# An attention kernel's score chunks: an even issue order, and the causal bar added by VectorE within its maximum

## The reference

```
Q, K, V = relu(xn @ W + b)                  # 16 heads of 8 channels
scores  = Q K^T / sqrt(8)                   # 512 x 512 per head and batch
scores  = -2^32 + 1 where the key is masked or lies behind the query
out     = softmax(scores) V + xn, then a layer norm with gamma and beta
```

## Time and profile before

| | us |
|---|---|
| median of three runs | 537.47 (536.09 to 538.89) |
| the profiled execution, its own time | 538.71 |
| its span in the trace | 536.9 |

### The profile page before, as it was taken

How to read it: one execution, slowest core, us unless ns; L and a number is a source line. 1 busy time by engine, 2 the same in 40 slices (tenths; PEclk the granted TensorE clock), 3 DMA queues, 4 the chain that set the end, 5 groups by cost and what they waited for, 6 DMA issues and landing times.

```text
span 536.9 us, 10757 instructions
## 1 busy us (share of the span) xinstructions
PE 447.4 (83%) x3773; PEld 275.3 (51%) x3773; DVE 406.4 (76%) x1008; ACT 315.3 (59%) x670; POOL 124.7 (23%) x345
## 2 busy tenths in 40 slices
PE   0049545988999739999999999999999999999981
PEld 0026334766777515565555555555556556556540
DVE  6898988887884238576977877877878878887715
ACT  0029135977888803566656666656667567566670
POOL 8000000000000011001045045045054063072181
PEclk9999958989999955799999999999999999999997
DMA  8900021223333351122122222322212213212000
GB/s 220 295 20 0 20 80 43 75 80 98 98 98 88 110 146 22 47 76 62 56 83 67 72 67 66 85 56 66 85 53 77 82 46 93 64 48 69 2 21 20
DMA packets 28585, 39.68 MB, mean 74 GB/s; under 512 B 5751, under 2 KB 19959, under 8 KB 28535
## 3 DMA queue, kind: packets, MB, share of 16 engines
q1 hardware_dynamic: 28486, 39.03, 26.0%
q10 hardware_dynamic: 48, 0.01, 0.0%
HBM read 25.91 MB, written 10.49 MB: 68 GB/s over the span
## 4 chain that ended last, share of the span: by engine, by line
PE 55%; DVE 6%; issue 1%; ACT 1%; DVEq 0%; ACTq 0%
PE banks L979 15%; PE banks L1010 14%; PE banks L998 13%; PE banks L981 6%; PE banks L1000 5%; DVE mx L837 3%; PE banks L1020 3%; DVE stats L879 1%; DVE aggr L883 1%; ACT pt L950 0%; ACT ots L934 0%; PE banks L988 0%; DVE res L866 0%; DVE res L869 0%; DVE mixed L870 0%
## 5 line engine op out<-in xcount | busy, mean ns | idle before, releaser
L837 DVE TENSOR_REDUCE mx<-banks 128x1 f32<-128x384 f32 (+3 forms) x384 | 212.5, 598 | 59.7 <-PE banks L981 52.5
L950 ACT ACTIVATE pt<-banks 128x512 f32<-128x512 f32 (+2 forms) x384 | 184.8, 528 | 110.4 <-PE banks L1000 104.1
L981 PE MATMUL banks<-causal,ident_b 128*128 128x128 bf16 x512 | 106.8, 228 | 0.0
L1000 PE MATMUL banks<-causalT,ident_b 128*128 128x128 bf16 x512 | 103.7, 222 | 0.0
L979 PE MATMUL banks<-w_room 73*128 73x512 bf16 (+3 forms) x256 | 75.3, 331 | 11.5 <-DVEq L912 10.3
L1010 PE MATMUL banks<-pt,vg 128*9 128x512 f32 (+3 forms) x1024 | 81.9, 438 | 0.5 <-ACT pt L950 0.5
L998 PE MATMUL banks<-w_room 76*128 76x512 bf16 (+3 forms) x256 | 71.2, 310 | 0.0
L979 PE MATMUL banks<-k_odd,q_odd 73*128 73x512 bf16 (+3 forms) x256 | 69.0, 302 | 1.6 <-DVE mx L837 1.6
L998 PE MATMUL banks<-q_odd,k_odd 76*128 76x512 bf16 (+3 forms) x256 | 67.6, 300 | 2.0 <-ACT pt L950 2.0
L750 POOL TENSOR_SCALAR mneg<-mx 128x16 f32<-128x16 f32 x32 | 8.1, 253 | 197.9 <-DVEq L845 197.9
L981 PEld LDWEIGHTS banks<-causal,ident_b 128*128 128x128 bf16 x512 | 52.1, 102 | 0.0
(11 more groups left out here) (155 smaller groups left out, 615.7 us busy)
## 6 DMA issues: line engine op xcount, KB each, us to landing
k_scratch<-parts SPq DMA_DIRECT2D x40, 128.0 KB, 2.3
w_room<-q_scratch SPq DMA_DIRECT2D x48, 96.0 KB
w_room<-k_scratch SPq DMA_DIRECT2D x48, 96.0 KB
q_odd<-q_scratch SPq DMA_DIRECT2D x48, 96.0 KB
k_odd<-k_scratch SPq DMA_DIRECT2D x48, 96.0 KB
q_scratch<-parts SPq DMA_DIRECT2D x24, 128.0 KB, 2.3
w_room<-in_w_dram SPq DMA_DIRECT2D x1, 2048.0 KB, 9.2
xn_all<-xn_st SPq DMA_DIRECT2D x8, 256.0 KB, 2.4
```

The source lines that it names most:

```text
L837: ins = dve.tensor_reduce(mx[:, u % 2, heads[0]:heads[-1] + 1, q], banks[:, S0 + c % RING, 0:w * len(heads)].rearrange("p (h k) -> p h k", ...
L950: act.activation(weights(k, heads[0], len(heads)), banks[:, ST0 + j % RING, 0:(T - P * k) * len(heads)], ACT.Exp, scale=SCALE).then_inc(ex ...
L981: ins = mm(o[:, w - P:w], ident_b[:, :], causal[:, :], start=False, stop=True)
L1000: ins = mm(o[:, 0:P], ident_b[:, :], causalT[:, :], start=False, stop=True)
```

## The change

Three things are edited:

- DVE's maximum of the eight single-head chunks becomes one `tensor_tensor_reduce`: it adds a row of `bars` to the chunk (in place, in PSUM) and gives the maximum of the sums. Pairs of heads keep the plain `tensor_reduce`.
- PE leaves the unit-matrix matmul out for those chunks.
- PE issues score chunk j right behind key chunk j for every j, ahead of the value products.

`bars` is a new [128, 512] bf16 tile, zero but for the bar in its last 128 columns, which POOL fills at the start; a chunk of width w takes its last w columns.

```diff
+    bars = sb("bars", [P, T], BF16)
...
+                pool.memset(bars[:, :], 0.0).then_inc(blank, 1)
...
+                pool.affine_select(out=bars[:, T - P:T], in_=bars[:, T - P:T], compare_op=ALU.is_ge, fill=-BIG, base=0,
+                                   pattern=[[-1, P]], channel_multiplier=1).then_inc(blank, 1)
...
                     dve.wait_ge(s_done, tok.next(s_done))
-                    ins = dve.tensor_reduce(mx[:, u % 2, heads[0]:heads[-1] + 1, q],
-                                            banks[:, S0 + c % RING, 0:w * len(heads)].rearrange(
-                                                "p (h k) -> p h k", k=w), AX.X, ALU.max)
+                    if len(heads) == 1:
+                        s = banks[:, S0 + c % RING, 0:w]
+                        ins = dve.tensor_tensor_reduce(s, s, bars[:, T - w:T], 1.0, -BIG, ALU.add, ALU.max,
+                                                       mx[:, u % 2, heads[0], q:q + 1])
+                    else:
+                        ins = dve.tensor_reduce(mx[:, u % 2, heads[0]:heads[-1] + 1, q],
+                                                banks[:, S0 + c % RING, 0:w * len(heads)].rearrange(
+                                                    "p (h k) -> p h k", k=w), AX.X, ALU.max)
...
-                        mm(o, qx[by][0:MROW + 1, g, h, P * q:P * q + P], kx[by][0:MROW + 1, g, h, 0:w],
-                           start=True, stop=False)
-                        ins = mm(o[:, w - P:w], ident_b[:, :], causal[:, :], start=False, stop=True)
+                        barred = len(heads) > 1
+                        ins = mm(o, qx[by][0:MROW + 1, g, h, P * q:P * q + P], kx[by][0:MROW + 1, g, h, 0:w],
+                                 start=True, stop=not barred)
+                        if barred:
+                            ins = mm(o[:, w - P:w], ident_b[:, :], causal[:, :], start=False, stop=True)
...
                             keys(tok, par, g, j)
+                            if ahead:
+                                if first and (g, j) == (2, 0):
+                                    pe.wait_ge(ones_in[1], 32)
+                                if j == 0:
+                                    loaded = stack_in[par if g + 2 < NG else 1 - par][(g + 2) % NG]
+                                    pe.wait_ge(loaded, tok.next(loaded, UNIT_DMAS))
+                                chunk(tok, par, g + 2, j)
                             if behind and j == 2:
                                 values(prev, 2)
                                 values(prev, 3)
                             if j == 10:
                                 values(g, 0)
                                 values(g, 1)
-                            for c in ((), (0,), (1,), (2, 3))[j] if j < 4 else (j,):
-                                if not ahead:
-                                    break
-                                if first and (g, c) == (2, 0):
-                                    pe.wait_ge(ones_in[1], 32)
-                                if c == 0:
-                                    loaded = stack_in[par if g + 2 < NG else 1 - par][(g + 2) % NG]
-                                    pe.wait_ge(loaded, tok.next(loaded, UNIT_DMAS))
-                                chunk(tok, par, g + 2, c)
```

More of the change, by code:

```diff
@@ L279, in _ @@
                 pool.memset(bias_rows[:, :, :], 0.0).then_inc(blank, 1)
-                pool.wait_ge(blank, 7)
+                pool.memset(bars[:, :], 0.0).then_inc(blank, 1)
+                pool.wait_ge(blank, 8)
                 for t in (ident, ident_b):
@@ L288, in _ @@
                 pool.memset(v_all[:, :, :], 1.0).then_inc(blank, 1)
-                pool.wait_ge(blank, 12)
+                pool.wait_ge(blank, 14)
                 pool.sem_inc(consts, 2)
@@ L310, in _ @@
                 pool.sem_inc(bias_ready, 1)
-                pool.sem_inc(blank, -12)
+                pool.sem_inc(blank, -14)
             @block.vector
```

## The result

The changed kernel takes 540.13 us (median of 16 runs, 538.62 to 541.39), the kernel before 537.32 (16 runs on the same chip, 535.79 to 538.89): a ratio of 1.005, 95% interval 1.0036 to 1.0063. It is slower by 2.8 us, though 256 matmuls are gone. The profiled execution took 540.98 us.

What follows compares the result with a forecast made beforehand. PE's in-order queue, held by ACT's chain in ordinary units and DVE in g = 1 units, was taken as bound; 0.9 + 3.1 + 1.2 - 0.9 = +4.3 us gave 543.0 profiled, 541.8 median, range 540 to 548.

Steps and rivals of the forecast that it cites:

- e: Excess time of DVE's new maximum over the old reduction, for occupancy and bank release alike: taken as 0.09 us.
- K7's wait: PE's idle time before key chunk 7's weights, waiting on ACT's exponential: to grow from 0.24 to about 0.8 us.
- K3 at 2.35: Key chunk 3 on PE starts 2.35 us behind the unit's first key chunk, 0.10 us later than before.
- Units with g = 1: Second unit of a batch, where DVE also does row statistics: +0.45 us each, +3.1 over seven, about 10.6 long.
- Ordinary unit: One group of four heads, first key chunk to the next unit's: 9.72 against 9.68 us, +0.9 over 22 units.
- K3 to K7: Stretch of PE's unit from key chunk 3 to key chunk 7, set by ACT's four steps: stays 2.50 us.
- The start of the part: Attention's start, where the first two units' maxima are made ahead on DVE: +1.4 less 0.2, so +1.2 us.
- the second rival: New maximum's excess near 0 (under 0.06 us): -0.8 to +2.7 us, 537 to 540, no change; chance 0.27.
- The cold unit: First attention unit (209 to 222 us), PE-bound at 1.2 GHz, where a bar takes twice 0.055: -0.9 us.
- The third rival: DVE becomes the bound, from an excess of 0.2 us on: 560 at 0.3, 610 at half rate; chance 0.10.
- POOL's extra steps: Extra fill and select at the program's start, beside load and norm of x; without that cover some 0.5 us.
- The first rival: Bars come off PE's path if ACT reaches key chunk 4's exponential sooner: 14.8 us go, 523; chance 0.10.

Runs made afterwards that it cites:

- the spread copies: Changed kernel with ACT's output copy (ots) behind exponential 2 and its transposed-maxima copy (mT) behind exponential 4, both formerly behind 3: 522.6 us; same edit on kernel before: 533.3.
- both edits: Changed kernel with ACT's two copies spread and DVE's row statistics moved: 517.1 us; in old order 531.2; kernel before with them 530.2, in even order 524.5.
- the move of two steps: ACT's copy of the transposed maxima (mT) moved from behind exponential 3 to behind 5: changed kernel 536.0 us, kernel before 534.1.

## Why the prediction was right, and where it was not

*The time.* 541.8 was forecast and 540.1 measured, slower as forecast, by 0.36 to 0.63%. That is just under the upper edge of what was called no change (540.2). That it came this near is in part luck: by the forecast's own sum, e = 0.05 us gives 0.9 + 1.5 + 0.6 - 0.9 = +2.1 us, 539.6. Another 0.33 us came at the start of the program, where nothing was added for it, and half a microsecond by which the medians differ more than the spans (2.8 against 2.28) is explained by no row.

*The signs.* K7's wait, the period of 9.7 us and K3 at 2.35 came as said. Units with g = 1 are 10.36 us and not 10.6, and two wide maxima 0.65 us apart and not 0.69; both fall short by the same e.

*Ordinary unit.* 2.36 + 2.50 + 4.86 = 9.72 was forecast, 2.35 + 2.51 + 4.85 = 9.71 measured. That ACT alone sets K3 to K7, and so hides the bars there, is shown by the spread copies: with nothing on PE or DVE changed this piece falls by 0.78 us. The wait at K7 was forecast at about 0.8 us: it shows as 0.90 ahead of the weights and 0.78 from start to start (0.95 less 0.17).

*The term that was mis-sized is e*, the excess of the new maximum: 0.09 us was taken, 0.05 measured in a chain, 0.02 behind a wait. With it the g = 1 term is -0.09 + 6 x 0.05 = +0.21 us, as measured, and 1.5 us in place of 3.1 over seven units. One of the seven was already at 10.42 before and gained nothing, so 1.2 came of it. The start of the part costs 0.6 in place of 1.2. I had taken e from small instructions behind one another (0.07 us each), but the accumulator read runs beside the next maximum. By its condition (e under 0.06) the second rival was the one that came; its own formula, -0.8 + 58e, gives +2.1 us at 0.05. The attention part measures +1.95 (2.28 less 0.33), the medians +2.8.

*The cold unit* gained 0.66 us of the 0.9 forecast; where the rest went was not looked for.

*The third rival* is out: e would have had to be 0.2, and no pass of half rate shows (716 ns for 512, 687 before). The rule of the Trainium skill (VectorE: DVE Perf Modes, Two Vector instructions with no wait between them) that the accumulator output makes a second instruction is seen in the trace: 256 of DVE_READ_ACCUMULATOR2_ANT, 142 ns each. The inference drawn from it, that the rival with e near 0 falls away, does not follow: of the 142 ns only 0.02 to 0.05 us shows from start to start.

*POOL's extra steps* were put at nothing, as lying beside the load and the norm of x, or at some 0.5 us without that cover. The cover does not hold: PE's first instruction comes 0.33 to 0.65 us later in every kernel with them, and 0.33 us is left of it at the start of the attention in these two profiles.

*The DMAs and the clock* did nothing that shows; the granted clock is 0.50 and 1.00 in the same stretches. One reading behind this was wrong: the last two units do not have half of the matmuls. The earlier trace rows give 140 in 15.4 us, so 70 a unit against about 100, and 9.1 per microsecond against 10.3.

*The first rival* was priced at 523 for the bars off the path; with ACT spread the changed kernel took 522.6. Its condition, ACT reaching K4's exponential within 1.95 us of K3, was the right one. That the number agrees is luck: its sum takes 0.48 us off each of 29 units, and what came off is 0.67 us in the 22 ordinary ones, while those with g = 1 grew by 0.2. What the prediction missed is that bars and order hang together there. With both edits the order is worth 6 us by itself, since it lets DVE work during V; taking the bars off PE is worth 7 more in the even order, and nothing in the old one.

## What to carry to other kernels

An edit that takes work from a busy engine pays only in the stretches that this engine ends: cut a period at each place where another engine releases it, and price the edit in each piece. When a large saving vanishes into such a wait, move what the releasing engine does first; here two copies shifted by one step each turned +2.8 us into -14.3. Before moving a copy, list who else waits for the bank that it reads: the move of two steps gave 0.50 us of a unit and took 0.34 back.

## What the runs showed of the hardware that was not expected

- An operation on DVE that takes PSUM and a bf16 row, writes the sum back in place and gives a maximum takes 716 ns for 128x512, 29 ns over the plain reduction, and 0.05 us more from start to start.
- The accumulator read behind it (142 ns) starts with the next operation of a chain. The bank's release is late by no more than the same 0.05: S8 of a unit with g = 1 stands at K0 + 6.67, six operations on, and 6.38 + 6e gives 0.05.
- In the eight kernels in which a small step of DVE (128x8, f32) met POOL's 3.94 us fill it took 0.72 to 0.93 us and ended with it; in the other six it took 0.17 us.
- The granted clock stayed at 0.50 from 196 to 222 us of the kernel before, although PE counts as busy 12.70 of the first 13 us and all of the 13 behind them, and was 1.00 from then on. No run here shows why.
- A PE that was busy all 258 us with 2777 matmuls kept its granted clock at 1.00, and so did the one with 5% fewer.
